# Four projections of a head pair in one slot, none in the next: a cross-attention block on one core

## The chip, the cores and the metric

The kernel runs on one core of one Trainium2 chip. The metric is the device time of one execution in microseconds (us); the time before is the median of three executions.

## The reference

The block takes x (4 batches, 1024 rows, 256 columns) and a context (4 batches, 64 rows, 192 columns) and computes, with 16 heads of 64:

```python
h = _ln(x, g1, be1)
x = _attn(h, h, Wq1, Wk1, Wv1, Wo1, bo1) + x          # self-attention, 1024 keys
h = _ln(x, g2, be2)
x = _attn(h, context, Wq2, Wk2, Wv2, Wo2, bo2) + x    # 64 keys
h = _ln(x, g3, be3)
a, gate = split(h @ Wp + bp)                          # 256 -> 2 x 1024
x = a * gelu(gate) @ W2 + b2 + x
```

In `_attn`, q, k and v are projections of h, the scores are `q k^T / 8`, softmax runs over the keys, and the heads' outputs go through Wo. Only the self-attention is touched by the change.

## The kernel before

Every float32 product that must be exact is made of three products of split operands (a leading part and a rest), listed in `TERMS`.

**Chunks.** The self-attention is a loop over 64 chunks C = 0 to 63, `for C in range(NC)`. A chunk is one pair of heads P = C // 2 and one half c = C % 2 of the 1024 queries, so each pair has a first chunk (C even, c = 0) and a second one (C odd, c = 1). A batch b has 16 chunks; n = C % 16 counts within it. In a chunk TensorE (PE) does, in this order:

1. Eight rounds, one for each tile of 128 keys. A round has eight score products on 64 rows of the array (`score`, L537 and L541) into the banks S0a and S0b (even rounds) or S1a and S1b (odd ones), and two products (`first_score`, L518) that give the row maxima of the next chunk, into T0 and PV or T1 and PJ.
2. In even chunks from C = 2 on, `sum_two(C - 2, "T0")` (L578): it sums what GpSimd has accumulated for chunks C - 2 and C - 1. It waits for `probs_added` to reach 7 C, that is for GpSimd's last addition of chunk C - 1.
3. Eight `attend` steps (L554): the exponentials times the values, in the bank that `products_bank(C)` names.
4. `whole_array(slot(C))`: the products that use the whole array of 128 x 128. This is "the slot".

**The slot.** `project_qk(P, u)` (L492) makes keys (u = 0 and 1, the two halves of the rows) or queries (u = 2 and 3) of pair P, six matmuls. Before the change a first chunk's slot makes u = 1 and 3 of the next pair, a second chunk's slot u = 0 and 2 of the pair after that. Eight `project_v` (L504) stand in the slots of C = 7, 15, ..., 55; out-projections (`out1`, L617) of the batch before in the slots with n = 1 and 2 of batches 1 to 3; and four transposes each of a normalised half (`turn_half`, L389) in the slots with n = 12 and 13. The normalised transposed input hT has two halves, and the projections of u = 1 and 3 read the second one, which the later of these slots renews for the next batch. That later slot is before the change n = 13, in batches 0 to 2.

**The other engines.** They run the same order of chunks, each in its own queue, and meet by semaphores. ScalarE (ACT) takes the exponential of each round (L1224), copies sums (L1291), makes the shift by the maxima (L1233), copies the chunk's products out of their bank (`write_oT`, L1247) and takes the leading part of each projection (L1205). VectorE (DVE) takes the row maxima (L882), inverts sums (L905) and takes the rest of each projection (L876); for a turned half it makes the rest of hT (L843). GpSimd (POOL) adds the exponentials of a chunk in seven additions (L1499 and L1502), scales the products of chunk C - 3 (`scale_oT`, L1508), and splits the weights of the pair after next (L1451, L1453). The exponentials lie in a ring of eight tiles, so GpSimd may be one chunk behind.

```python
for C in range(NC):
    for jt in range(TILES): ...        # scores, first scores
    if C and C % 2 == 0:
        sum_two(C - 2, "T0")
    for jt in range(TILES):
        attend(TILES * C + jt)
    whole_array(slot(C))
```

Of the kernel before, what the change touches and what calls it, by code (L numbers as in the profile page):

```python
# [48 lines left out]
def block_kernel(nc, x, ctx, Wq1, Wk1, Wv1, Wo1, bo1, Wq2, Wk2, Wv2, Wo2, bo2, Wp, bp, W2, b2,  # L49
                 g1, be1, g2, be2, g3, be3, out):  # L50
    B, N, DIM = x.shape
# [9 lines left out]
    KT = DIM // PART  # L61
    PAIRS = HEADS // 2
    TILES = N // PART
    CHUNKS = N // BANK
# [6 lines left out]
    BC = PAIRS * CHUNKS  # L71
    NC = B * BC
# [10 lines left out]
    with stack:  # L83
# [6 lines left out]
        def overlay(*specs):  # L90

            with ExitStack() as scope:
# [44 lines left out]
        qk = (qk0, qk1)  # L137


        _, *places = overlay(("oT_kept", [PRING, N], F32),  # L140
                             *((f"oT_part{n}", [PAIRS, PART], F32R) for n in range(4)))
        oT_parts = (places[0:2], places[2:4])

        _, wo1_last, oT_last_hi, _, oT_last_lo = overlay(
            ("before_vT", [(PRING + TILES) * N], F32), ("wo1_last", [2, PAIRS, DIM], F32R),
            ("oT_last_hi", [PAIRS, PART], F32R), ("acc_between", [N], F32), ("oT_last_lo", [PAIRS, PART], F32R))
# [54 lines left out]
        turned = ((turned0, turned_lo0), (turned1, turned_lo1), (turned2, turned_lo2))  # L201
# [120 lines left out]
        def next_norm(b, c):  # L322

            return (1, CHUNKS * (b + 1) + c) if b + 1 < B else (2, c)

        def slot(C):


            P, c = divmod(C, CHUNKS)
            (b, n), D = divmod(C, BC), C // (4 * CHUNKS)  # L330
            jobs, between = [], []
            if n - BC + 4 in range(CHUNKS if b + 1 < B else 1):
                between += [("ln", next_norm(b, n - BC + 4), k) for k in range(KT)]
            if C % (4 * CHUNKS) == 4 * CHUNKS - 1 and D + 1 < GROUPS:
                between += [("v", D + 1, jt) for jt in range(TILES)]

            through = ("PV", "T0") if between and between[0][0] == "ln" else ("PV", "S0b", "S1a")
            jobs += [(*job, through[i % len(through)]) for i, job in enumerate(between)]
            after = P + 1 + c
            if after < B * PAIRS:  # L340
                jobs += [("qk", after, 1 - c, "S1b"), ("qk", after, 3 - c, "PJ")]
            return jobs + [("out1", *tile, through[i % len(through)]) for i, tile in enumerate(out1_tiles(C))]

        def out1_tiles(C):

            b, n = divmod(C, BC)
            return [(b - 1, TPC * (n - 1) + t) for t in range(TPC)] if b and n in (1, 2) else []
# [11 lines left out]

        def products_bank(C):  # L360

            return "S0a" if C + 3 < NC else "T0" if C + 2 < NC else "PV"


        LAST = range(3, TILES)
# [9 lines left out]
        def _(e):  # L375
# [3 lines left out]
            def bank_free(*names):  # L379
                for name in names:  # L380
                    for semaphore, value in free[name]:
                        need.wait_ge(semaphore, value)
# [15 lines left out]
            def normed(key):  # L398
                need.wait_ge(s.hT_hi, turned_by(key))
                need.wait_ge(s.hT_lo, turned_by(key))  # L400
# [84 lines left out]
            def project_qk(P, u, bank="PJ"):  # L485
                kind, c = (1 if u < 2 else 0), u % 2
                need.wait_ge(s.wqk_split, 2 * (P + 1))
                normed((1, P // PAIRS * CHUNKS + c))
                bank_free(bank)
                for i, (w, h) in enumerate(TERMS):  # L490
                    for k in range(KT):
                        last = e.matmul(banks[bank], wqk[:, P % 2, w, kind, k, :],  # L492
                                        hT[:, h, k, c * BANK:(c + 1) * BANK],
                                        start=(i == k == 0), stop=(i == 2 and k == KT - 1))
                last.then_inc(s.qk_projected, 1)
                free[bank] = ((s.split_lo, qk_of[P, u]),)
# [47 lines left out]
            def attend(R):  # L544
                C, jt = R // TILES, R % TILES
                D, p = C // (4 * CHUNKS), C // CHUNKS % 4
                need.wait_ge(s.v_copied, TILES * D + jt + 1)
                need.wait_ge(s.exponential, R + 1)
                bank = products_bank(C)
                if jt == 0:  # L550
                    bank_free(bank)
                for head in range(2):
                    c0 = p * PART + head * DH
                    last = e.matmul(banks[bank][head * DH:(head + 1) * DH, :], vT[:, v_slot(D, jt), c0:c0 + DH],  # L554
                                    pT[:, jt, head, :], start=(jt == 0), stop=(jt == TILES - 1))
                last.then_inc(s.attended, 1)
                if jt == TILES - 1:
                    free[bank] = ((s.oT_written, C + 1),)
# [171 lines left out]
            for i in range(TILES):  # L730
                project_v(0, i, ("S0a", "S0b", "S1a", "S1b")[i % 4])
            project_qk(0, 3, "PJ")
            project_qk(1, 0, "S1a")
            project_qk(1, 2, "S1b")
            for C in range(NC):
                for jt in range(TILES):
                    if C == NC - 1 and jt == TILES - 2:

                        sum_keys(C - 1, "T0")
                    for part in range(len(TERMS) + 1):  # L740
                        for head in range(2):
                            score(TILES * C + jt, part, head)
                    if C + 1 < NC:
                        for head in range(2):
                            first_score(*next_part(C + 1, jt), head)
# [5 lines that stand above are left out]
# [31 lines left out]
        def _(e):  # L782
            need = Waits(e)

            def ln_stats(src, mv_of, key):

                n, slot = stat_of[key], key[1] % TILES
                need.wait_ge(s.ln_agg, n - TILES if n > TILES else 0)
                e.bn_stats(stats[:, slot, :], src).then_inc(s.ln_stats, 1)
                need.wait_ge(s.ln_stats, n)  # L790
                e.bn_aggr(mv_of, stats[:, slot, :]).then_inc(s.ln_agg, 1)
# [79 lines left out]
            def split_qk(P, u, bank="PJ"):  # L871
                kind, c = (1 if u < 2 else 0), u % 2
                span = slice(c * BANK, (c + 1) * BANK)
                need.wait_ge(s.split_hi, qk_of[P, u])
                hi, lo = (qk[P % 2][:, 2 * kind + w, span] for w in range(2))
                e.scalar_tensor_tensor(lo, banks[bank], SCALE if kind == 0 else 1.0, hi.bitcast(F32),  # L876
                                       ALU.mult, ALU.subtract).then_inc(s.split_lo, 1)
# [144 lines left out]
            gather_max(0)  # L1022
            turn_max(0)
            split_qk(0, 3, "PJ")
            split_qk(1, 0, "S1a")
            split_qk(1, 2, "S1b")
            for C in range(NC):
                b, n = divmod(C, BC)
                if C + 1 < NC:
# [27 lines left out]
            for i in range(NT + 3):  # L1057
# [10 lines left out]
                if i in (TPC + 1, 2 * TPC + 1):  # L1068

                    c = i // TPC + 1  # L1070
# [27 lines left out]
        def _(e):  # L1098
# [101 lines left out]
            def split_qk(P, u, bank="PJ"):  # L1200
                kind, c = (1 if u < 2 else 0), u % 2
                need.wait_ge(s.qk_projected, qk_of[P, u])
                if P >= 2:
                    need.wait_ge(s.scored, 4 * TILES * (P - 1))
                e.activation(qk[P % 2][:, 2 * kind, c * BANK:(c + 1) * BANK], banks[bank], ACT.Copy,  # L1205
                             scale=SCALE if kind == 0 else 1.0).then_inc(s.split_hi, 1)
# [30 lines left out]
            def write_oT(C):  # L1237
                P, c = C // CHUNKS, C % CHUNKS
                need.wait_ge(s.attended, TILES * (C + 1))
                need.wait_ge(s.values2_stored, 16)  # L1240
                if P >= PRING - 2:
                    need.wait_ge(s.wo1_stored, 16)
                if P >= PRING:

                    b = (P - PRING) // PAIRS
                    need.wait_ge(s.out1_product, TILES * b + TPC * (c + 1))
                e.copy(oT[:, P % PRING, c * BANK:(c + 1) * BANK], banks[products_bank(C)]).then_inc(s.oT_written, 1)  # L1247
# [132 lines left out]
                    fetch_table(ACT.Exp, 1)  # L1380
            make_shift(0)
            split_qk(0, 3, "PJ")
            split_qk(1, 0, "S1a")
            split_qk(1, 2, "S1b")
            for C in range(NC):
                b, n = divmod(C, BC)
                norm_chunk = norm1 if b + 1 < B else norm2
# [426 lines left out]
```

## Time and profile before

| | |
|---|---|
| median of 3 executions | 2012.57 us (2011.95 to 2013.1) |
| the profiled execution, its own time | 2013.08 us |
| its span, first to last instruction | 2011.3 us |
| busy PE, DVE, ACT, POOL | 2006.6, 1448.6, 1270.5, 1488.9 us |
| granted TensorE clock | 1.00 over the span |

Busy time is the time in which at least one instruction of that engine ran. Matmuls overlap, so the pace of TensorE is read from the distance between the starts of its instructions, not from their durations. Times in the rows are counted from the start of the span.

### The profile page before, as it was taken

What the parts mean: (1) busy time and instruction counts of PE and PEld (TensorE: products, weight loads), DVE (VectorE), ACT (ScalarE), POOL (GpSimd) and SP (SyncE); (2) the same over time, 40 slices, a digit from 0 to 9 for tenths busy, and PEclk for the clock granted to TensorE, in tenths of its full rate; (3) what the DMA queues carried; (4) which work ended last, traced back from release to release, by engine and by line L of the source; (5) the groups of instructions that cost most, each with busy time, mean ns of one, the idle gap of its engine ahead of it and who ended that gap; (6) DMA issues with size and microseconds to landing.
All of it is one profiled execution on the core that took longest, in us unless ns stands there. A gap on an engine that the chain in (4) does not pass through costs nothing.

```text
span 2011.3 us, 33039 instructions
## 1 busy us (share of the span) xinstructions
PE 2006.6 (100%) x12696; PEld 1379.4 (69%) x12696; DVE 1448.6 (72%) x2575; ACT 1270.5 (63%) x2164; POOL 1488.9 (74%) x796
## 2 busy tenths in 40 slices
PE   9999999999999999999999999999999999999999
PEld 7655655666565556765665666565559999888888
DVE  6588688677868886588688667768877888744443
ACT  6576677665667776566678665667766767533332
POOL 2799799978989998899899888989897665300000
DMA  7201000001000000010000001000030520000100
GB/s 274 85 33 37 6 7 16 7 26 48 17 11 6 17 7 27 1 64 7 6 7 22 27 1 50 9 27 1 22 96 11 157 74 1 1 22 22 43 11 32
DMA packets 48958, 67.22 MB, mean 33 GB/s; under 512 B 6176, under 2 KB 42144, under 8 KB 46752
## 3 DMA queue, kind: packets, MB, share of 16 engines
q1 hardware_dynamic: 48800, 65.10, 10.1%
q8 instruction: 100, 1.64, 0.3%
q14 instruction: 58, 0.48, 0.1%
HBM read 45.17 MB, written 19.92 MB: 32 GB/s over the span
## 4 chain that ended last, share of the span: by engine, by line
PE 97%; POOL 2%; issue 0%; ACT 0%; DVE 0%; POOLq 0%
PE score L554 21%; PE score L537 18%; PE score L692 9%; PE score L541 6%; PE score L492 5%; PE attn_project L677 5%; PE attn_project L706 5%; PE attn_project L492 4%; PE score L647 4%; PE first_score L518 4%; PE score L504 3%; PE attn_project L518 2%; PE score L617 2%; PE attn_project L617 2%; POOL acc L1502 2%; PE attn_project L504 2%
## 5 line engine op out<-in xcount | busy, mean ns | idle before, releaser
L1502 POOL TENSOR_TENSOR acc<-acc,pT 128x1024 f32<-128x1024 f32 x384 | 917.7, 2390 | 53.8 <-POOL acc L1502 0.4
L1224 ACT ACTIVATE pT<-score 128x1024 f32<-128x1024 f32 x512 | 525.3, 1027 | 133.2 <-PE score L541 92.6
L537 PE MATMUL score<-qk 64*128 64x512 f32 x3072 | 457.2, 399 | 0.4 <-ACT pT L1224 0.4
L554 PE MATMUL score<-pT,vT 128*64 128x512 f32 x1952 | 432.3, 595 | 0.0
L882 DVE TENSOR_REDUCE nmax<-first_score 128x1 f32<-128x512 f32 x512 | 347.8, 679 | 5.0 <-PE first_score L518 2.9
L882 DVE TENSOR_REDUCE nmax<-attn_project 128x1 f32<-128x512 f32 x512 | 347.0, 678 | 0.0
L537 PEld LDWEIGHTS score<-qk 64*128 64x128 f32 x3072 | 257.7, 184 | 118.6 <-ACT pT L1224 67.1
L554 PEld LDWEIGHTS score<-pT,vT 128*64 128x64 f32 x1952 | 134.8, 137 | 280.1 <-issue 243.8
L905 DVE RECIPROCAL sums<-sums 128x512 f32<-128x512 f32 (+1 forms) x65 | 214.7, 3303 | 5.7 <-ACT sums L1291 1.6
L876 DVE SCALAR_TENSOR_TENSOR qk<-score,qk 128x512 fp32r<-128x512 f32 x66 | 45.5, 690 | 225.1 <-ACT qk L1205 225.1
L541 PE MATMUL score<-shift,pick 64*128 64x512 f32 x1024 | 206.1, 391 | 0.0
L518 PE MATMUL first_score<-qk 64*128 64x512 f32 x512 | 200.7, 392 | 0.0
L518 PE MATMUL attn_project<-qk 64*128 64x512 f32 x512 | 200.6, 392 | 0.0
L1499 POOL TENSOR_TENSOR acc<-pT 128x1024 f32<-128x1024 f32 x64 | 152.8, 2387 | 53.4 <-ACT pT L1224 53.4
L692 PE MATMUL score<-hT,wp 128*128 128x512 f32 x768 | 184.1, 396 | 0.0
L1489 POOL TENSOR_TENSOR xres<-xres,rows 128x1024 f32<-128x1024 f32 x8 | 19.2, 2401 | 203.1 <-DVE xn L813 203.1
L692 PEld LDWEIGHTS score<-hT,wp 128*128 128x128 f32 x768 | 142.4, 188 | 31.9
L1291 ACT COPY sums<-first_score 32x512 f32<-32x512 f32 x248 | 142.9, 576 | 9.4 <-PE first_score L578 6.4
L541 PEld LDWEIGHTS score<-shift,pick 64*128 64x128 f32 x1024 | 100.0, 184 | 21.0 <-ACT shift L1233 0.2
L1539 POOL TENSOR_TENSOR probs<-probs,rsum 128x1024 f32<-128x1024 f32 x32 | 61.0, 1907 | 65.9 <-DVE rsum L944 65.9
L898 DVE STREAM_TRANSPOSE maxima_T<-maxima 32x32 f32<-32x32 f32 x512 | 103.5, 202 | 8.3
L1233 ACT ACTIVATE shift<-maxima_T,mask 128x128 fp32r<-128x128 f32 x256 | 81.7, 390 | 43.7 <-DVE maxima_T L898 43.0
(195 smaller groups left out, 3119.1 us busy)
## 6 DMA issues: line engine op xcount, KB each, us to landing
xres<-x_middle SPq DMA_DIRECT2D x10, 512.0 KB, 3.6
raw_qk<-in_L_xattn_Wq SPq DMA_DIRECT2D x32, 128.0 KB, 2.2
raw_qk<-in_L_xattn_Wk SPq DMA_DIRECT2D x32, 128.0 KB, 2.4
raw_v<-in_L_xattn_Wv SPq DMA_DIRECT2D x8, 512.0 KB, 4.6
keys_all<-keys SPq DMA_DIRECT2D x1, 4096.0 KB, 13.0
values_all<-values SPq DMA_DIRECT2D x1, 4096.0 KB, 12.4
out_x<-xres SPq DMA_DIRECT2D x7, 512.0 KB, 2.9
xres<-in_x SPq DMA_DIRECT2D x3, 1024.0 KB, 7.0
```

The costliest lines, as they stand in the source:

```text
L492: last = e.matmul(banks[bank], wqk[:, P % 2, w, kind, k, :], hT[:, h, k, c * BANK:(c + 1) * BANK], start=(i == k == 0), stop=(i == 2 and k ...
L518: last = e.matmul(banks[bank], qk[P % 2][r, w, q0:q0 + PART], qk[P % 2][r, 2 + h, half * BANK:(half + 1) * BANK], start=(m == 0), stop=(m ...
L537: e.matmul(bank, qk[P % 2][r, 2 + h, keys], qk[P % 2][r, w, queries], start=(part == 0), stop=False)
L541: e.matmul(bank, pick[r, :], shift[r, :], start=False, stop=True).then_inc(s.scored, 1)
L554: last = e.matmul(banks[bank][head * DH:(head + 1) * DH, :], vT[:, v_slot(D, jt), c0:c0 + DH], pT[:, jt, head, :], start=(jt == 0), stop=( ...
L692: last = e.matmul(banks[bank], wp[q][:, w, k, which, o:o + PART], hT[:, h, k, (c % 2) * BANK:(c % 2 + 1) * BANK], start=(term == k == 0), ...
L882: e.tensor_reduce(nmax[:, head, t, half:half + 1], banks[PASS_BANKS[head][half]], AX.X, ALU.max, negate=True).then_inc(s.row_max, 1)
L905: e.reciprocal(sums[:, C % 2, part], sums[:, C % 2, part]).then_inc(s.sum_inverse, len(halves))
L1224: e.activation(pT[:, jt].rearrange("p h n -> p (h n)"), SC[R % 2][:, :], ACT.Exp).then_inc(s.exponential, 1)
L1291: last = e.copy(sums[r * DH // 2:(r + 1) * DH // 2, o, :], banks[bank][g * DH // 2:(g + 1) * DH // 2, :])
L1499: e.tensor_tensor(total, pT[:, jt - 1], pT[:, jt], ALU.add).then_inc(s.probs_added, 1)
L1502: e.tensor_tensor(total, total, pT[:, jt], ALU.add).then_inc(s.probs_added, 1)
```

## The change

`slot(C)` gives a first chunk all four projections of the next pair and a second chunk none. In the slots with n = 12 and now n = 14 (no longer 13) the transposes of the next batch's input go with them, each time through PV and T0: at n = 12 behind u = 0 and 2, at n = 14 ahead of all four. The two projections of pair 1 that stood ahead of the loop are gone, on all three engines. The last two of eight value projections go through PV and PJ. A chunk with an empty slot puts its attention products in T0 instead of S0a.

```diff
             P, c = divmod(C, CHUNKS)
             (b, n), D = divmod(C, BC), C // (4 * CHUNKS)
-            jobs, between = [], []
-            if n - BC + 4 in range(CHUNKS if b + 1 < B else 1):
-                between += [("ln", next_norm(b, n - BC + 4), k) for k in range(KT)]
+            jobs = []
             if C % (4 * CHUNKS) == 4 * CHUNKS - 1 and D + 1 < GROUPS:
-                between += [("v", D + 1, jt) for jt in range(TILES)]
-
-            through = ("PV", "T0") if between and between[0][0] == "ln" else ("PV", "S0b", "S1a")
-            jobs += [(*job, through[i % len(through)]) for i, job in enumerate(between)]
-            after = P + 1 + c
-            if after < B * PAIRS:
-                jobs += [("qk", after, 1 - c, "S1b"), ("qk", after, 3 - c, "PJ")]
-            return jobs + [("out1", *tile, through[i % len(through)]) for i, tile in enumerate(out1_tiles(C))]
+                jobs += [("v", D + 1, jt, ("PV", "S0b", "S1a", "PV", "S0b", "S1a", "PV", "PJ")[jt]) for jt in range(TILES)]
+            if c == 0 and P + 1 < B * PAIRS:
+                turned = n - BC + 4
+                norm = ([("ln", next_norm(b, turned // 2), k, ("PV", "T0")[k]) for k in range(KT)]
+                        if turned == 0 or turned == 2 and b + 1 < B else [])
+                jobs += norm if turned == 2 else []
+                jobs += [("qk", P + 1, 0, "S0b" if norm else "PV"), ("qk", P + 1, 2, "S1a" if norm else "T0")]
+                jobs += norm if turned == 0 else []
+                jobs += [("qk", P + 1, 1, "S1b"), ("qk", P + 1, 3, "PJ")]
+            return jobs + [("out1", *tile, ("PV", "S0b", "S1a")[i % 3]) for i, tile in enumerate(out1_tiles(C))]
...
-            return "S0a" if C + 3 < NC else "T0" if C + 2 < NC else "PV"
+            return "S0a" if slot(C) else "T0" if C + 2 < NC else "PV"
...
             project_qk(0, 3, "PJ")
-            project_qk(1, 0, "S1a")
-            project_qk(1, 2, "S1b")
```

The two lines that went from `project_qk` went from `split_qk` on VectorE and on ScalarE as well.

## Rows read from the trace of the kernel before

**Rows 1.** The page: busy time of two engines, and the chain that ended last.

```profile
PE 2006.6 (100%) x12696; PEld 1379.4 (69%) x12696; DVE 1448.6 (72%) x2575; ACT 1270.5 (63%) x2164; POOL 1488.9 (74%) x796
PE 97%; POOL 2%; issue 0%; ACT 0%; DVE 0%; POOLq 0%
```

**Rows 2.** The waits of PE: us in total, times, longest us.

```profile
PE score L537 <- ACT pT L1224: 0.4, 2, 0.2
```

**Rows 3.** Timeline of PE, end of chunk 5: start us, us, line, count.

```profile
168.76 7.09 PE L554 MATMUL score<-pT,vT 128*64 128x512 f32 x32
175.78 1.66 PE L492 MATMUL score<-hT,wqk 128*128 128x512 f32 x6
177.28 1.56 PE L492 MATMUL attn_project<-hT,wqk 128*128 128x512 f32 x6
178.78 0.96 PE L537 MATMUL score<-qk 64*128 64x512 f32 x6
```

**Rows 4.** Timelines of PE, ACT and DVE, chunk 61, which has an empty slot.

```profile
1446.82 7.09 PE L554 MATMUL first_score<-pT,vT 128*64 128x512 f32 x32
1453.84 0.96 PE L537 MATMUL score<-qk 64*128 64x512 f32 x6
...
1453.96 0.59 ACT L1247 COPY oT<-first_score 128x512 f32<-128x512 f32 x1 [1.87 <-PE first_score L554]
...
1446.09 0.68 DVE L882 TENSOR_REDUCE nmax<-first_score 128x1 f32<-128x512 f32 x1
```

**Rows 5.** Timeline of PE, inside the slot of chunk 23.

```profile
595.71 1.56 PE L492 MATMUL score<-hT,wqk 128*128 128x512 f32 x6
597.11 1.56 PE L492 MATMUL attn_project<-hT,wqk 128*128 128x512 f32 x6
```

**Rows 6.** Timelines of PE and POOL, chunk 20.

```profile
507.15 0.96 PE L537 MATMUL score<-qk 64*128 64x512 f32 x6
...
516.71 1.06 PE L578 MATMUL first_score<-acc,ones 128*32 128x512 f32 x8
...
527.71 0.96 PE L537 MATMUL score<-qk 64*128 64x512 f32 x6
...
502.68 12.54 POOL L1502 TENSOR_TENSOR acc<-acc,pT 128x1024 f32<-128x1024 f32 x5
```

**Rows 7.** The same places of chunks 22, 36 and 14, PE and POOL.

```profile
556.84 1.06 PE L578 MATMUL first_score<-acc,ones 128*32 128x512 f32 x8
...
544.65 10.03 POOL L1502 TENSOR_TENSOR acc<-acc,pT 128x1024 f32<-128x1024 f32 x4
...
885.13 1.07 PE L578 MATMUL first_score<-acc,ones 128*32 128x512 f32 x8
...
871.29 12.53 POOL L1502 TENSOR_TENSOR acc<-acc,pT 128x1024 f32<-128x1024 f32 x5
...
362.12 1.06 PE L578 MATMUL first_score<-acc,ones 128*32 128x512 f32 x8
...
342.00 15.03 POOL L1502 TENSOR_TENSOR acc<-acc,pT 128x1024 f32<-128x1024 f32 x6
```

**Rows 8.** Timelines of PE and DVE, chunks 13 and 14, and the start of 15.

```profile
331.77 0.96 PE L537 MATMUL score<-qk 64*128 64x512 f32 x6
...
348.47 0.66 PE L389 MATMUL attn_project<-ident,xn 128*128 128x128 f32 x4
...
349.32 1.64 PE L492 MATMUL score<-hT,wqk 128*128 128x512 f32 x6
...
373.12 0.96 PE L537 MATMUL score<-qk 64*128 64x512 f32 x6
...
352.32 0.69 DVE L843 TENSOR_TENSOR hT<-first_score,hT 128x512 fp32r<-128x512 f32 x1
```

**Rows 9.** Timeline of PE, the starts of chunks 0 and 1.

```profile
59.11 0.97 PE L537 MATMUL score<-qk 64*128 64x512 f32 x6
...
78.96 0.97 PE L537 MATMUL score<-qk 64*128 64x512 f32 x6
```

More of the change, by code:

```diff
@@ L1024, in _ @@
             split_qk(0, 3, "PJ")
-            split_qk(1, 0, "S1a")
-            split_qk(1, 2, "S1b")
             for C in range(NC):
@@ L1382, in _ @@
             split_qk(0, 3, "PJ")
-            split_qk(1, 0, "S1a")
-            split_qk(1, 2, "S1b")
             for C in range(NC):
```

## The prediction

> **What bounds the kernel now.** I read the page first: TensorE is busy 2006.6 of 2011.3 us and holds 97% of the chain that ended last, while GpSimd is busy 1488.9 us [rows 1]. GpSimd works almost only in the attention loop, so there it is close behind. Then the waits: the longest entry inside the loop is 0.4 us in all [rows 2]. So a change pays if TensorE's own sequence gets shorter, and costs where it makes TensorE wait for something that is now just in time. Both are read from the timelines, from the starts of instructions, since durations of matmuls overlap.
>
> **What a projection costs.** In an ordinary second chunk the first projection starts 7.02 us after the first attend, the second 1.50 later, the next scores 1.50 after that [rows 3]. In the middle of a longer slot the distance of two projections is 1.40 [rows 5]. So a slot costs 0.10 on the way in and 0.10 on the way out beyond 1.40 for each projection. Chunk 61 has an empty slot already: from its first attend to the next scores 7.02 us pass [rows 4], as many as to a projection [rows 3]. So going from attends straight to scores costs nothing more than going to a projection, and an emptied slot gives back 3.00.
>
> The Trainium skill (TensorEngine Tiling (Array Packing), Key Properties) says that changing the tiling mode drains TensorE. This kernel has three modes, 64 x 128, 128 x 64 and 128 x 128, and by the rule the direct way from attends to scores is a change too, so one drain of two would go and an emptied slot would save 0.10, not 0.20. Both ways leave an attend after the same 7.02 us, whatever follows, so the trace prices the direct change inside the 7.02 and I take 0.20.
>
> **The sum, part by part.**
>
> 1. *Slots.* 31 first chunks (C = 0 to 60) get two projections more, at 1.40 each: +2.80. Thirty second chunks (C = 1 to 59) lose theirs. Ten of them keep a slot, seven with value projections and three with out-projections; they lose 2.80 and cancel against their neighbour. Seventeen become empty: 3.00 - 2.80 = 0.20 each, 3.4 us less. Three (C = 13, 29, 45) are in item 3. The two projections ahead of the loop cancel against the slot of chunk 0. Between 0 and 0.20 for each of the seventeen bounds this term: 0 to -3.4; I take -3.4, since chunk 61 is the very situation.
>
> 2. *Start.* Chunk 0 takes 19.85 us from its first scores to those of chunk 1 [rows 9], where an even one without a sum of keys should take 7.02 + 3.00 and eight rounds of 1.19 (chunk 20 needs 9.56 for eight [rows 6]), 19.58. The difference is the wait for the banks S1a and S1b, which the two projections ahead of it filled. That goes: -0.3, with 0 as the other end.
>
> 3. *Transposes of the next batch.* They move from n = 13 to n = 14, where projections of u = 1 and 3 stand behind them, which read what they make. Now, the second half of hT is finished at 352.32 + 0.69 = 353.01, and the slot began at 348.47 [rows 8]: 4.54 us. After the change the slot of C = 14 holds the transposes (349.32 - 348.47 = 0.85), two projections that need only the first half (1.50 and 1.40), and is then at 3.75: TensorE waits until 4.54 and for the semaphore (0.05 lie between the end of a maximum, 1446.77, and the attends that waited for it, 1446.82 [rows 4]), some 0.84. The slot of C = 13 began 16.70 after its scores [rows 8]; empty, the chunk is 16.7 long. An even chunk's slot begins 20.56 - 3.00 = 17.56 after its scores [rows 6]. So chunk 14 takes 17.56 + 3.75 + 0.84 + 2.90 = 25.05, both 41.75, against 373.12 - 331.77 = 41.35: +0.4 in each of three batches, +1.2. If VectorE is not free at once, 1 us more each; if the wait doesn't appear, 0.84 less each: bounds -1.3 to +4.2.
>
> 4. *The sum of keys.* This is the part that speaks against the change. TensorE now comes to a first chunk's scores 3.00 us earlier in relation to GpSimd, because the second chunk has become short, while GpSimd's work in a chunk is what it was. `sum_two` of chunk C waits for GpSimd's last addition of chunk C - 1. In chunk 20 that addition ends at 502.68 + 12.54 = 515.22 and the sum starts at 516.71 [rows 6]: 1.49 to spare. After the change the sum would be due 3.00 earlier, so TensorE waits 1.51, and about 0.1 for the semaphore. GpSimd can't move with it: it has no pause in these rows, and what last held it to TensorE, the out-projections in the slot of chunk 18, stand at the same time as before (slot 17 is 2.8 shorter, slot 18 2.8 longer). In chunk 36 the spare time is 885.13 - 883.82 = 1.31 [rows 7], in chunk 52 it is the same within 0.02: 1.7 and 0.1 each. Together 1.6 + 1.8 + 1.8 = +5.2.
>
>  It doesn't repeat in the next pairs. Before, GpSimd comes nearer to TensorE from chunk 20 to 22: its additions end 554.67 - 515.22 = 39.45 apart and the sums start 40.13 apart [rows 6, 7], and the spare time grows to 2.17 [rows 7]. After the change the sum of chunk 22 is due 3.0 + 0.2 earlier and 1.6 later for the wait in chunk 20: 0.6 to spare. Chunk 14 has 362.12 - 357.03 = 5.09 [rows 7], of which 3.00 + 0.85 go with the slot of chunk 13 and its transposes and 0.4 with two emptied slots before it: 0.8 left. The slots with eight value projections then let GpSimd catch up, but what TensorE has waited is lost, since it has no pause elsewhere. What is behind the waiting sum: the attends, ScalarE's eight copies of the sums, the shift by the maxima. The shift is due in the first round of the next chunk, behind the attends and four projections (7.02 + 5.8 us), in which ScalarE has nothing else that is long; they move together with the sum, so nothing more is late. Bounds of this term: 0 if GpSimd gained what TensorE gained, and 12 if the 0.6 and 0.8 didn't hold and two further sums in each batch waited about 1.
>
> 5. *The bank T0.* In a chunk with an empty slot, the attends write T0. It must be free of VectorE's maxima before, and copied by ScalarE before the next chunk's second score step. In chunk 61 the maximum of T0 ends at 1446.77 and the attends start at 1446.82; the copy ends at 1454.55, 0.71 after the next scores started at 1453.84, and T0 is wanted behind the first eight products, of which six alone take 0.96 [rows 4]. So both are just in time there: 0, and if VectorE or ScalarE were later by a quarter of a microsecond, 20 chunks would pay up to 0.25: +5.
>
> 6. *Queues.* SyncE's loads and GpSimd's splitting of weights keep their places; the weights of a pair are used one slot later than now. Nothing on the path.
>
> Sum: -3.4 - 0.3 + 1.2 + 5.2 = +2.7 us. On the profiled execution's own time, 2013.08, this gives 2015.8; that execution lies 0.5 above the median of 2012.57, so on the median it is **2015.3 us**, 0.13% more. About 0.2%, 4 us, is what a measurement of this kernel can tell from no change.
>
> **The rivals.**
>
> *A, my forecast:* the emptied slots pay 3.7 and the three late sums and three turned halves eat it up, 2015.3. Chance 0.50, its own range 2013 to 2017.5.
>
> *B, faster:* GpSimd keeps its distance. Then nothing is left but -3.4 - 0.3 + 1.2 = -2.5: 2010.1; without the wait of item 3 as well, 2007.5. Against it: the 1.49 and 1.31 us are smaller than the 3.00 by which the sum moves. It decides where the spare time of [rows 6] is over 3 us; for it speaks only that GpSimd's ends in a profile may be late by a few tenths. Chance 0.15, a third of it below 2008.5.
>
> *C, slower, the two engines locked:* the pair of chunks costs GpSimd 39.45 us [rows 6, 7] and TensorE then 40.13 - 0.20 = 39.93. That is 0.5 apart; a little more on GpSimd's side, and each first chunk of a stretch waits again. With two further sums of 1 us in each of three batches: 2015.3 + 6 = 2021. Chance 0.15.
>
> *D, slower, T0:* item 5 costs 0.25 in 20 chunks, 2015.3 + 5 = 2020.3. Against it: chunk 61 shows none of it. For it: only one such chunk is in the trace. Chance 0.10.
>
> *E, by the rule of modes:* a direct change costs its own 0.10, so an emptied slot saves 0.10: 2015.3 + 1.7 = 2017.0. If it saves nothing, 2018.7. Chance 0.10. The page is the one named above, TensorEngine Tiling (Array Packing) in the Trainium skill; the trace doesn't agree so far, since chunk 61 leaves after 7.02.
>
> **Numbers.** Faster by over 0.2% (below 2008.5): a third of B and a little of A, 0.07. Slower by over 0.2% (above 2016.6): C and D, half of E and a fifth of A, 0.35 less what of them stays small, 0.33. The rest is 0.60. The range, from 2009.5 to 2020.3, leaves out the low end of B and most of C.
>
> **What would show it.** Right: in the waits of PE, L578 (the sum) waiting for POOL L1502 some three times, 1.5 to 1.8 us each, at chunks 20, 36 and 52; a projection in the slots of chunks 14, 30 and 46 waiting 0.9 us for VectorE's rest of hT; second chunks of 16.54 us, first ones of 23.4. Item 1 is wrong if an emptied second chunk is longer than 16.6. Item 5 is wrong if L554 or L518 wait in chunks after or in an empty slot. Item 4 is wrong if L578 waits nowhere, or in over three chunks, or if the waits are far from 1.6 us.

## The result, and the profile after

| | before | after |
|---|---|---|
| median, 18 runs each | 2012.78 us (2011.95 to 2013.52) | 2016.49 us (2015.61 to 2017.17) |
| ratio | | 1.0018, 95% interval 1.0011 to 1.0025 |
| span of the profiled execution | 2011.3 us | 2014.8 us |
| busy PE | 2006.6 us | 2003.1 us |

The change makes the kernel 3.7 us slower, 0.18%. The prediction was 2015.3 us, 2.7 us more than before, for the reasons of case A; the measured median is 1.2 us above it, of which 0.2 are the median before, 2012.78 us in 18 runs instead of 2012.57 in three. TensorE is busy 3.5 us less and the span is 3.5 us longer, so some 7 us of pause have come into its queue. The profile names them: 4.7 + 2.4 us in the first two rows below.

The waits of PE after the change (us in total, times, longest us), which answer to [rows 2]:

```profile
PE first_score L581 <- POOL acc L1499: 4.7, 3, 1.7
PE score L495 <- DVE hT L844: 2.4, 3, 0.8
PE score L410 <- POOL ones L1564: 0.9, 1, 0.9
PE attn_project L592 <- POOL oT L1505: 0.5, 1, 0.5
PE score L540 <- ACT pT L1223: 0.4, 2, 0.2
```

Two rows are new, and they are the two that the prediction worked out: the sum of keys waiting for GpSimd three times, and a projection waiting for the rest of hT three times. The granted clock is 1.00 over the span, as before.

Timelines of PE and of POOL in chunk 20, which answer to [rows 6] (L581 is the sum of keys, L557 the attends, L495 the projections):

```profile
503.24 0.96 PE L540 MATMUL score<-qk 64*128 64x512 f32 x6
...
514.27 1.06 PE L581 MATMUL first_score<-acc,ones 128*32 128x512 f32 x8 [1.41 <-POOL acc L1499]
515.26 7.09 PE L557 MATMUL score<-pT,vT 128*64 128x512 f32 x32
522.28 1.66 PE L495 MATMUL attn_project<-hT,wqk 128*128 128x512 f32 x6
523.78 1.56 PE L495 MATMUL first_score<-hT,wqk 128*128 128x512 f32 x6
525.18 1.56 PE L495 MATMUL score<-hT,wqk 128*128 128x512 f32 x6
526.58 1.56 PE L495 MATMUL attn_project<-hT,wqk 128*128 128x512 f32 x6
528.08 0.96 PE L540 MATMUL score<-qk 64*128 64x512 f32 x6
```

```profile
501.71 12.50 POOL L1499 TENSOR_TENSOR acc<-acc,pT 128x1024 f32<-128x1024 f32 x5
```

GpSimd's additions of chunk 19 end at 514.21, and the sum starts at 514.27. Before the change they ended 1.49 us ahead of it. GpSimd ends 1.0 us earlier than before in absolute time, TensorE's scores start 3.9 us earlier. From one to the next, and on to the scores of chunk 21, the four projections take 1.50, 1.40, 1.40 and 1.50 us.

A whole second chunk with an empty slot, chunk 5, from its first scores to those of chunk 6 (PE):

```profile
158.14 0.96 PE L540 MATMUL score<-qk 64*128 64x512 f32 x6
...
174.71 0.96 PE L540 MATMUL score<-qk 64*128 64x512 f32 x6
```

It takes 16.57 us; before it took 178.78 - 159.21 = 19.57 (its end is in [rows 3], this is its start):

```profile
159.21 0.96 PE L537 MATMUL score<-qk 64*128 64x512 f32 x6
```

The slot of chunk 14 on PE, which answers to [rows 8], and what its third projection waited for on DVE:

```profile
364.52 0.66 PE L392 MATMUL attn_project<-ident,xn 128*128 128x128 f32 x4
365.01 0.60 PE L392 MATMUL first_score<-ident,xn 128*128 128x128 f32 x4
365.37 3.04 PE L495 MATMUL score<-hT,wqk 128*128 128x512 f32 x12
369.20 1.63 PE L495 MATMUL score<-hT,wqk 128*128 128x512 f32 x6 [0.79 <-DVE hT L844]
```

```profile
368.36 0.69 DVE L844 TENSOR_TENSOR hT<-first_score,hT 128x512 fp32r<-128x512 f32 x1
```

The rest of hT is finished 4.53 us after the slot began (369.05 - 364.52); 4.54 was read before.

**The account.** The starts of the chunks in the two traces, subtracted, give each term of the prediction's sum. They add up to the 3.5 us by which chunk 63 starts later. The first two rows are together item 1 of the prediction, -3.4 forecast and -2.6 measured.

| term | predicted | measured |
|---|---|---|
| 1. seventeen emptied slots | -3.4 | -2.8 |
| 1. ten slots that keep value or out-projections | 0 | +0.2 |
| 2. start, to the scores of chunk 1 | -0.3 | -0.7 |
| 3. transposes, three batches | +1.2 | +1.9 |
| 4. sum of keys, three waits | +5.2 | +4.9 |
| 5. T0 in chunk 61 | 0 | +0.1 |
| sum | +2.7 | +3.5 |

### The profile page after: what moved, and what is told of

Its sections match the earlier page's. It is cut to its first block, busy times and chain, and to the rows that moved or that the text cites. A ratio compares the mean times of both kernels' runs of the same rounds, so it can differ in the third digit from the quotient of the medians.

```text
span 2014.8 us, 33084 instructions
## 1 busy us (share of the span) xinstructions
PE 2003.1 (99%) x12696; PEld 1378.9 (68%) x12696; DVE 1451.4 (72%) x2575; ACT 1270.0 (63%) x2164; POOL 1488.7 (74%) x796
## 4 chain that ended last, share of the span: by engine, by line
PE 92%; POOL 6%; issue 1%; ACT 1%; DVE 0%; DMA 0%; POOLq 0%; DVEq 0%
PE score L540 16%; PE score L557 14%; PE score L695 9%; PE first_score L557 6%; PE score L544 5%; PE attn_project L680 5%; PE attn_project L709 5%; PE score L650 4%; PE attn_project L495 4%; POOL acc L1499 4%; PE first_score L521 4%; PE score L495 3%; PE score L507 3%; PE attn_project L507 2%; PE attn_project L521 2%; PE first_score L495 2%
## 5 line engine op out<-in xcount | busy, mean ns | idle before, releaser
L557 PE MATMUL score<-pT,vT 128*64 128x512 f32 x1312 | 290.6, 595 | 0.0
L557 PEld LDWEIGHTS score<-pT,vT 128*64 128x64 f32 x1312 | 90.6, 137 | 193.1 <-issue 166.4
L557 PE MATMUL first_score<-pT,vT 128*64 128x512 f32 x672 | 148.8, 595 | 0.0
L877 DVE SCALAR_TENSOR_TENSOR qk<-attn_project,qk 128x512 fp32r<-128x512 f32 x56 | 38.7, 691 | 100.7 <-ACT qk L1204 100.7
```

## Experiments

The letters here and in the expectations stand for the cases of the experiments, and are not those of the prediction. The theory (A): TensorE gains 0.2 us in each emptied slot, but its sum of keys is bound to GpSimd, whose total of work over a stretch of chunks is nearly TensorE's own; and a projection now follows too closely on the transposes that it reads. The rivals: the wait is a local lateness only (B), or isn't GpSimd's (C). Line numbers in the edits are left out; all kernels compute the whole block.

### GpSimd's split of the value weights, two and three chunks later

In chunk 19, ahead of the sum of chunk 20, GpSimd also splits the value weights of the next group, two instructions of 3.5 us in all; the same split stands ahead of the sums of chunks 4, 12, 28, 36, 44 and 52. What sets chunks 20, 36 and 52 apart in the trace is that two chunks earlier GpSimd also works for the out-projections of the batch before, with a pause of 5.9 to 6.2 us in which it waits for ScalarE. The sums of chunks 4, 12, 28 and 44 don't wait after the change; GpSimd is done with their additions 1.6 to 2.1 us ahead. These two kernels move the split.

```diff
-                if C % (4 * CHUNKS) == 3 and C // (4 * CHUNKS) + 1 < GROUPS:
+                if C % (4 * CHUNKS) == 5 and C // (4 * CHUNKS) + 1 < GROUPS:
                     split_wv(C // (4 * CHUNKS) + 1)
```

> GpSimd splits the value weights at chunks with C % 8 == 5 (5, 13, 21, ...) instead of 3 (3, 11, 19, ...); all else as after the change. The split is 3.5 us of GpSimd's time. Theory A (GpSimd is behind over the whole stretch from chunk 19 to 23, the wait is owed to the total of its work): the waits of the sum of keys at chunks 20, 36 and 52 go (4.7 us in all), but with TensorE 1.6 us earlier the sums of chunks 22, 38 and 54 wait instead, about 1.1 us each, 3.3 in all: 2016.5 - 1.5 = 2015.0. Rival B (the wait is a local lateness, owed to the split standing just before chunk 20): all waits go, 2011.7. Rival C (the wait is not GpSimd's): 2016.5.

Measured: 2015.03 us (11 runs), 1.5 less than after the change. The waits of PE for it:

```profile
PE first_score L581 <- POOL acc L1499: 2.2, 2, 1.2
PE first_score L581 <- DVE nmax L883: 1.5, 1, 1.5
```

Three waits of the sum are left, at chunks 22, 38 and 54, 3.7 us where 3.3 was expected. Chunk 20 and chunk 22 on PE:

```profile
512.57 1.07 PE L581 MATMUL first_score<-acc,ones 128*32 128x512 f32 x8
...
553.55 1.06 PE L581 MATMUL first_score<-acc,ones 128*32 128x512 f32 x8 [0.99 <-POOL acc L1499]
```

The wait has gone from chunk 20 and come up in chunk 22. A cleared wait buys only 0.5 us when the engine that was waited for has no slack over the next pair. B fell.

The profile puts one of the three waits, that of chunk 38, down to DVE. The sum waits for both engines, since T0 must be free as well, so the engine that was done last is read from the timelines (PE, POOL and DVE):

```profile
923.50 1.06 PE L581 MATMUL first_score<-acc,ones 128*32 128x512 f32 x8 [1.52 <-DVE nmax L883]
...
908.40 15.04 POOL L1499 TENSOR_TENSOR acc<-acc,pT 128x1024 f32<-128x1024 f32 x6
...
922.19 0.68 DVE L883 TENSOR_REDUCE nmax<-first_score 128x1 f32<-128x512 f32 x1
```

VectorE's last maximum of T0 ends at 922.87, GpSimd's last addition at 923.44, 0.06 us ahead of the sum. So this wait too is for GpSimd.

The second kernel has 6 in place of 5, so the split stands behind the last sum of the stretch.

> The same split at chunks with C % 8 == 6, so behind the sums of chunks 6, 14, 22, ...; it is needed only in the slot of the next chunk. Theories A and B alike: no sum of keys waits any more, 4.7 us less than after the change, 2011.8. Rival C (the wait is not GpSimd's): 2016.5, with the sum still waiting. Theory D (the whole loss of the change is this wait, and the rest is a gain): then it is faster than the kernel before by about 1 us (2012.8 before).

Measured: 2011.13 us (11 runs), ratio to before 0.9993 (0.9984 to 1.0002), 5.4 less than after the change. No sum waits, and the only wait that the change has left is this one:

```profile
PE score L495 <- DVE hT L844: 2.4, 3, 0.8
```

In chunk 20 the additions now end ahead of the sum again (PE and POOL):

```profile
512.47 1.06 PE L581 MATMUL first_score<-acc,ones 128*32 128x512 f32 x8
...
502.95 7.50 POOL L1499 TENSOR_TENSOR acc<-acc,pT 128x1024 f32<-128x1024 f32 x3
```

They end at 510.45, 2.0 us ahead. C fell with it. What D says holds in its direction: this kernel is 1.5 us faster than the one before, but the interval of the ratio still includes no difference.

### The sum of keys 3.5 us later, GpSimd untouched

```diff
-                if C and C % 2 == 0:
+                if C and C % 2 == 0 and C not in (20, 22, 36, 38, 52, 54):
                     sum_two(C - 2, "T0")
                 for jt in range(TILES):
+                    if jt == 4 and C in (20, 22, 36, 38, 52, 54):
+                        sum_two(C - 2, "T0")
                     attend(TILES * C + jt)
```

> As after the change, but in chunks 20, 22, 36, 38, 52 and 54 the sum of keys stands behind the fourth attend instead of ahead of the first, 3.5 us later. GpSimd is not touched. Theory A: the sum is then due at 13.1 us after the chunk's first scores and the additions end at 10.9 to 11.2, so nothing waits: 4.7 us less, 0.1 to 0.2 us more in each of the six for going from attends to the sum and back, net 4: 2012.5. Rival (GpSimd's lateness shows elsewhere once the sum doesn't wait for it, in the exponentials or the attends): little gain, 2015 to 2016.5.

Measured: 2012.73 us (11 runs), 3.8 less than after the change. No sum waits for GpSimd; the attends of chunks 36 and 52 wait 0.5 us for the exponentials in all. So it is the due time of that one consumer which counts, not GpSimd's lateness in itself.

### The same move of the split in the kernel before

The edit is that of the second kernel above (6), on the kernel before the change.

> The kernel before the change with the split of the value weights at C % 8 == 6 instead of 3. Theory: before the change the sum of chunk 20 had 1.49 us to spare, so GpSimd's lateness cost nothing and moving the split brings nothing: 2012.7, same. Rival (the split itself was slowing something before too, and its move is a gain for any order of projections): 2009 to 2011.

Measured: 2012.39 us (11 runs), ratio 0.9999 (0.9990 to 1.0007). The move is worth 5.4 us after the change and nothing before it: the wait is made by the change.

### GpSimd one instruction longer in chunks 19, 35 and 51

```diff
+                if D in (3, 5, 7):
+                    e.tensor_tensor(wv[:, 1].rearrange(flat)[:, 0:BANK], raw_v[:, :, :].rearrange(flat)[:, 0:BANK],
+                                    raw_v[:, :, :].rearrange(flat)[:, 0:BANK], ALU.subtract)
                 split_weights(raw_v[:, :, :].rearrange(flat), wv[:, 0].rearrange(flat), wv[:, 1].rearrange(flat),
```

> As after the change, with one more GpSimd instruction of about 1.3 us (a subtraction of 512 columns, overwritten at once) ahead of the split of the value weights in chunks 19, 35 and 51. Theory: GpSimd's time in these stretches is on the path one for one, so the waits of the sums of chunks 20, 36 and 52 grow from 1.4 to 1.7 us to 2.7 to 3.0, +3.9: 2020.4 if TensorE's clock stays. In the run with the transposes alone at n = 13 a pause of 2.46 us was followed in two of three places by a stretch at granted clock 0.50 that cost 1.5 to 2.8 us; if that happens here in one to three places, 2022 to 2029. Rival (GpSimd's lateness there is not what the sum waits for): 2016.5.

Measured: 2022.65 us (4 runs, 2019.93 to 2023.08), 6.2 more than after the change. The instruction took 1.04 us, not 1.3, and the waits grew by 2.7 us in three places:

```profile
PE first_score L581 <- POOL acc L1502: 7.4, 3, 2.5
```

So GpSimd's time there is on the path nearly one for one: 2.7 of 3.1 us. The other 3.5 us are nearly all TensorE's clock. In two of the three places, chunks 20 and 52, it fell at about the end of the pause. These chunks take 27.28 and 27.75 us, against 24.84 and 25.08 after the change; chunk 36, with the same pause and no fall, takes 26.10 against 25.08. Stretches of the profiled execution about chunk 20 (time; busy PE, PEld, DVE, ACT, POOL; then the granted clock, DMA share, GB/s):

```profile
512.00:515.40 3.40, 0.97 (x14) 0.46 (x12) 3.29 (x10) 1.02 (x2) 3.26 (x3) 0.94 0.00 0
515.40:518.00 2.60, 2.60 (x10) 0.46 (x12) 0.93 (x5) 1.65 (x3) 2.52 (x3) 0.50 0.00 0
518.00:522.00 4.00, 4.00 (x20) 1.36 (x18) 2.20 (x1) 3.92 (x7) 3.86 (x3) 0.95 0.54 149
```

```profile
515.36 1.94 PE L581 MATMUL first_score<-acc,ones 128*32 128x512 f32 x8 [2.42 <-POOL acc L1502]
```

The sum itself takes 1.94 us there, against 1.06 in chunk 20 after the change.

### The attention products of a chunk with an empty slot in S0a

```diff
-            return "S0a" if slot(C) else "T0" if C + 2 < NC else "PV"
+            return "S0a" if C + 3 < NC else "T0" if C + 2 < NC else "PV"
```

> As after the change, but chunks with an empty slot keep their attention products in S0a, as before the change. Theory: nothing stands any more between the last attend and the next chunk's first scores, which write S0a; they wait until ScalarE has copied it, 0.12 + 0.59 + 0.05 = 0.76 us in each of 20 chunks, 15.2, less 2.3 that the sums of chunks 20, 36 and 52 then wait less: 2016.5 + 13 = 2029.5. Rival (the bank is of no account, the first scores would be held by something else): 2016.5.

Measured: 2028.73 us (4 runs). The waits of PE for it:

```profile
PE score L540 <- ACT oT L1246: 13.7, 20, 0.7
PE score L495 <- DVE hT L844: 2.4, 3, 0.8
PE first_score L581 <- POOL acc L1499: 1.5, 2, 0.9
PE first_score L581 <- DVE nmax L883: 0.9, 1, 0.9
```

Twenty waits of 0.7 us, 13.7 in all, and the three sums wait 2.4 us where they waited 4.7, since TensorE now comes later to them. That leaves 11.4 of the 12.2 us by which this kernel is slower than the one after the change. The slot's projections had been the cover of ScalarE's copy. T0 takes their place, and without it the change would cost some 16 us instead of 3.7.

### One tiny matmul on the whole array in each emptied slot

```diff
                 whole_array(slot(C))
+                if C < NC - 3 and not slot(C):
+                    bank_free("PV")
+                    e.matmul(banks["PV"][:, 0:64], pick[:, :], pick[:, 0:64], start=True, stop=True)
```

It stands in the kernel with the change and the split at 6 (2011.13).

> The kernel with the change and the split at C % 8 == 6 (2011.13), and one matmul of 64 columns on the whole array in each of the 20 emptied slots, its result unused. It streams some 0.03 us. By the rows (a direct way from attends to scores costs nothing extra, a way through the whole array 0.10 in and 0.10 out): 20 x 0.23 = +4.6, 2015.7. By the rule that each change of mode drains the array (the direct way costs one drain of 0.10, the detour two): 20 x 0.13 = +2.6, 2013.7. If the emptied slots gain nothing from the modes: +0.6, 2011.7.

Measured: 2015.69 us (11 runs), 4.6 more, as the rows say and not as the reading of the rule would have it. Its first such place, chunk 5 (PE):

```profile
174.86 0.30 PE L754 MATMUL attn_project<-pick 128*128 128x64 f32 x1
175.09 0.98 PE L540 MATMUL score<-qk 64*128 64x512 f32 x6
```

The matmul puts 0.23 us between the attends and the next scores. So a visit to the whole array costs 0.20 apart from its work, and the direct way from attends to scores costs nothing that the 7.02 us of the attends don't hold already. This takes the matmul's own share to be the 0.03 us of its columns; what else so short a matmul may cost was not measured apart. The starts of the projections give the same 0.20 without it: 1.50 at either end of a slot, 1.40 within.

### The transposes back in the slot with n = 13

Alone there, with the four projections left at n = 14:

```diff
+            turned = n - BC + 4
+            if turned == 1 and b + 1 < B:
+                jobs += [("ln", next_norm(b, 1), k, ("PV", "T0")[k]) for k in range(KT)]
             if c == 0 and P + 1 < B * PAIRS:
...
-                        if turned == 0 or turned == 2 and b + 1 < B else [])
+                        if turned == 0 else [])
-                jobs += norm if turned == 2 else []
```

> As after the change, but the second pair of transposes of the next batch stays in the slot with n = 13, where it stood before, as that slot's only work; the slot with n = 14 has the four projections alone. Theory: the wait of a projection for the rest of hT (2.4 us in three batches) goes; the slot of chunk 13 costs one way out of the whole array more (0.1) and chunk 14's rounds are 0.27 longer, as before. Net 0.5 us less in each batch, 1.6 in all: 2014.9. Rival (the transposes block T0 or PV for the next chunk's first scores when no projection stands behind them): the wait moves into the scores of chunk 14, no gain or a loss of about 1 us each.

Measured: 2023.99 us (5 runs, 2021.32 to 2025.92), 7.5 more where 1.6 less was expected. The rival was right: with nothing behind the transposes the next chunk's first scores wait for T0, and for longer than the projection did: 2.5 us each time instead of 0.8. Waits, and the first place on PE (chunk 14):

```profile
PE first_score L522 <- DVE hT L845: 7.4, 3, 2.5
```

```profile
348.63 0.40 PE L545 MATMUL score<-shift,pick 64*128 64x512 f32 x2
351.49 0.46 PE L522 MATMUL first_score<-qk 64*128 64x512 f32 x1 [2.46 <-DVE hT L845]
```

In the profiled execution, the slowest of the five with 2025.92 us, these waits are 5.0 us more than the 2.4 that they replace. The clock takes some 4.3 more, in two of three places: chunks 14, 30 and 46 take 26.06, 28.88 and 27.58 us with the same pause. About chunk 30:

```profile
721.00:723.00 2.00, 0.00 (x0) 0.00 (x0) 1.97 (x3) 1.40 (x2) 1.86 (x2) 0.89 0.00 0
723.00:726.00 3.00, 2.79 (x14) 2.42 (x16) 1.35 (x3) 0.25 (x1) 2.86 (x2) 0.50 0.00 0
726.00:729.00 3.00, 3.00 (x18) 2.54 (x16) 2.01 (x4) 1.80 (x2) 3.00 (x3) 0.50 0.01 3
729.00:732.00 3.00, 3.00 (x28) 2.35 (x24) 2.54 (x5) 2.04 (x2) 2.92 (x5) 0.93 0.08 25
```

The second try gives the transposes their cover back: n = 13 and n = 14 hold what they held before the change, on top of the split at 6.

```diff
+            if n == BC - 3 and b + 1 < B:
+                jobs += [("ln", next_norm(b, 1), k, ("PV", "T0")[k]) for k in range(KT)]
+                jobs += [("qk", P + 2, 0, "S1b"), ("qk", P + 2, 2, "PJ")]
+            if n == BC - 2 and b + 1 < B:
+                jobs += [("qk", P + 1, 1, "S1b"), ("qk", P + 1, 3, "PJ")]
-            if c == 0 and P + 1 < B * PAIRS:
+            elif c == 0 and P + 1 < B * PAIRS:
...
-                        if turned == 0 or turned == 2 and b + 1 < B else [])
+                        if turned == 0 else [])
-                jobs += norm if turned == 2 else []
```

> The kernel with the change and the split at C % 8 == 6 (2011.13), and the slots with n = 13 and 14 of batches 0 to 2 as before the change: transposes and two projections at n = 13, two projections at n = 14. Theory: the wait of 0.8 us for the rest of hT goes; the pair of chunks takes 41.35 us as before instead of 41.96: 0.6 less in three batches, 1.8 in all, 2009.3. Rival (the wait only moves to the first scores, as with the transposes alone at n = 13): 2011 or more.

Measured: 2009.52 us (11 runs, 2008.59 to 2010.07), ratio to the kernel before 0.9984 (0.9975 to 0.9993). It beats both kernels, by 3.2 us and by 7.0. The 3.2 us are about what the emptied slots and the start give in the account (2.6 + 0.7), with nothing lost to waits. No wait inside the attention loop of more than 0.4 us in all is left in its profile.

## Why the prediction was right, point by point

The time came out 1.0 us more above the kernel before than forecast (3.7 for 2.7), by the mechanism of case A. In the spans the miss is 0.8 us, and it is a sum of larger ones that partly cancel: item 1 is off by 0.8, item 3 by 0.7, items 2 and 4 by -0.4 and -0.3.

**Slots (item 1): right, a little smaller.** An emptied slot gives back 2.94 to 3.03 us where 3.00 was forecast, and a filled one takes 2.80. Seventeen pairs gain 2.8, not 3.4, and the ten that keep other work lose 0.2. By the prediction's own mark (an emptied chunk of over 16.6 us) one of the seventeen, chunk 11 with 16.62, is just beyond it; the others are at 16.55 to 16.59. The price of 0.20 for a visit to the whole array was taken from chunk 61 alone; the tiny matmul confirmed it 20 times over (+4.6 for a forecast of +4.6). Of the missing 0.6, 0.25 lie in the four first chunks with n = 12, where transposes stand in the slot too: they grow by 2.83 to 2.88 instead of 2.80. The rest, 0.02 in each pair, was not traced to a cause. Rival E fell. Key Properties in TensorEngine Tiling (Array Packing) of the Trainium skill says that a change of mode drains the array. With one drain of 0.10 for each change of mode, the tiny matmuls would have cost 2.6 us, not 4.6. (The prediction counts three modes; the sum of keys is a fourth, 128 x 32, and item 1 doesn't touch it.) The traces agree with the page for the way into and out of the whole array, 0.10 each, and for the way from attends to scores it is either inside the 7.02 us of the attends or not there.

**Start (item 2): right in kind.** Chunk 0 takes 22.41 us, where 19.58 + 2.80 = 22.38 should remain with its waits gone. The other 0.45 lies ahead of the loop, where the change does nothing: the last projection ahead of it already starts at 54.36, before at 54.81. That stretch varies: chunk 0 starts at 59.11 us in the profiled execution before the change and at 57.98 with the value weights' split moved, which changes nothing there, while from the scores of chunk 0 to those of chunk 63 the same two take 1412.28 and 1412.26 us. So the 0.45 can't be told from scatter; without it item 2 measured -0.25.

**Transposes (item 3): the mechanism right, the size too small.** The wait is 0.79 us for a forecast of 0.84, three times. But chunks 13 and 14 take 16.78 + 25.18 = 41.96 us, not 41.75. The prediction took the wait to cost what its length is, and it costs 0.2 us more. The profile counts the wait from the end that it gives to the twelve matmuls before it, 365.37 + 3.04 = 368.41, but in a row without a pause the third projection would start at 365.37 + 1.50 + 1.40 = 368.27, so the pause is 0.93 us by the starts; and the third projection takes 1.47 after it, not 1.40. This term is 0.7 of the miss, second to item 1.

**Sum of keys (item 4): right in place, number and size.** Three waits, at chunks 20, 36 and 52, of 1.48, 1.72 and 1.72 us in the length of the chunk, for a forecast of 1.6, 1.8 and 1.8. Chunks 22 and 14 don't wait; GpSimd is done 0.46 and 0.78 us ahead of their sums, where 0.6 and 0.8 were worked out. The two positions of the value weights' split confirmed the part that is easy to overlook: GpSimd's pair of chunks and TensorE's are within half a microsecond of each other, so the lateness isn't cured by moving work within the stretch, only by moving it out.

**T0 (item 5): right.** Rival D fell: the emptied chunks don't wait for T0 by more than 0.07. The kernel with S0a shows what it would be without.

Rival C, the two engines locked over more pairs, did not appear after the change. It is near: with the split moved from chunk 19 to 21, the wait at chunk 20 was gone and chunk 22 waited.

**The chances.** The prediction's chance of being slower by over 0.2% is added up wrongly: C, D, half of E and a fifth of A are 0.40, not 0.35. The measured 2016.49 us lies just under the 2016.6 that it counts from.

## What to carry to other kernels

A change that leaves each engine's work as it is can still move one engine's due times against another's. Read the spare time of each handshake at the places where the producer is latest, and compare it with the shift: here 1.3 to 1.5 us against 3.0 in three of 31 sums. Three more (chunks 22, 38 and 54) had 1.9 to 2.2 us, less than the shift as well, and don't wait only because TensorE has just waited at the sum before. Then ask whether the producer's pace over the next stretch gives the wait back; if not, clearing one wait only passes it on, and the work has to leave the stretch. And work that stands between a producer and a bank's next use is cover: before taking it away, look for what it hid.

## What the runs showed of the hardware that was not expected

A pause of TensorE can cost the clock as well. Around pauses of 1.4 to 1.7 us (after the change, three places) the granted clock stayed at 1.00. Around pauses of 2.42 to 2.5 us it fell to 0.50, the level of 1.2 GHz, in two of three places in each of two profiled executions, with TensorE busy without a break before each pause. It fell at about the end of the pause. What made the difference between the four places and the two others of the same length, no run here shows. It came back some 6 us later at chunk 30 of the one kernel and sooner at chunk 20 of the other. In that chunk 30 the scores from the pause to the sum took 2.8 us more than in chunk 14 of the same execution, which had the same pause without the fall. The two kernels with such pauses also have the widest spread of times, 4.6 us in five runs and 3.2 in four, where the others lie within 1.6 us.
